# Attention and feed-forward block: work regrouped into three phases, with the maxima transposed on VectorE

## The reference

```python
q = (x @ wq).reshape(bsz, toks, 32, 16)      # 32 query heads of size 16
k = (x @ wk).reshape(bsz, toks, 8, 16)       # 8 key/value groups, 4 query heads each
v = (x @ wv).reshape(bsz, toks, 8, 16)
scores = einsum('bqgrd,bkgd->bgrqk', qg, k) / sqrt(16)
out = einsum('bgrqk,bkgd->bqgrd', softmax(scores), v).reshape(bsz, toks, 512) @ wo
x = layernorm(x + out)
inter = x @ c1_w.T @ c2_w.T                  # rank 16, 1792 columns in blocks of 32
idx = argmax of each block of 32             # one column of each block is kept
h = relu(x . w1[idx]);  out = h @ w2t[idx]
x = layernorm(x + out)
```

## Time and profile before

| | |
|---|---|
| median of 3 runs | 1001.59 us (998.66 to 1003.35) |
| profiled execution | 998.58 us, of which the span from first to last instruction is 996.8 us |
| mean granted TensorE clock | 0.944 of full |
| PE busy | 908.2 us (91%) |
| DVE busy | 562.4 us (56%) |
| ACT busy | 442.9 us (44%) |
| POOL busy | 193.1 us (19%) |
| DMA | 92.99 MB |

### The profile page before, as it was taken

How to read it: one execution, slowest core, us unless ns; L and a number is a source line. 1 busy time by engine, 2 the same in 40 slices (tenths; PEclk the granted TensorE clock), 3 DMA queues, 4 the chain that set the end, 5 groups by cost and what they waited for, 6 DMA issues and landing times. The chain is left out here.

```text
span 996.8 us, 12134 instructions
## 1 busy us (share of the span) xinstructions
PE 908.2 (91%) x4472; PEld 533.0 (53%) x4472; DVE 562.4 (56%) x743; ACT 442.9 (44%) x821; POOL 193.1 (19%) x183
## 2 busy tenths in 40 slices
PE   5868999999899998999989975999999999999995
PEld 3745543333334333343333434777777777777774
DVE  4636567888656885468866533545563365326413
ACT  3302466777654775456765542322222222222231
POOL 6302003730210002100021002333321222122221
PEclk8889999999989998599988978999999999999998
DMA  8466535643342243323433124214030002001101
GB/s 249 160 205 240 169 110 159 175 123 91 91 117 69 76 134 80 97 85 79 135 82 109 34 97 102 82 44 155 14 116 11 1 3 103 2 1 43 42 1 42
DMA packets 50858, 92.99 MB, mean 93 GB/s; under 512 B 5648, under 2 KB 13840, under 8 KB 50288
## 3 DMA queue, kind: packets, MB, share of 16 engines
q1 hardware_dynamic: 49312, 87.05, 29.3%
q0 software_dynamic: 1488, 5.16, 1.9%
HBM read 56.80 MB, written 34.87 MB: 92 GB/s over the span
## 5 line engine op out<-in xcount | busy, mean ns | idle before, releaser
L509 DVE TENSOR_REDUCE neg_max<-ps_max 128x2 f32<-128x1024 f32 x256 | 302.9, 1217 | 90.1 <-PE ps_max L670 89.7
L486 ACT ACTIVATE probs<-ps_st 128x512 f32<-128x512 f32 x496 | 270.2, 595 | 142.6 <-PE ps_st L707 139.7
L707 PE MATMUL ps_st<-q,k 50*128 50x512 f32 x496 | 181.9, 511 | 28.5 <-ACT probs L486 27.6
L707 PEld LDWEIGHTS ps_st<-q,k 50*128 50x128 f32 x496 | 71.9, 192 | 203.1 <-ACT probs L486 156.8
L670 PE MATMUL ps_max<-k,q 48*128 48x512 f32 x512 | 152.8, 452 | 14.0 <-DVE neg_max L509 9.2
L721 PE MATMUL ps_pv<-probs,v 128*32 128x512 f32 x1024 | 147.3, 649 | 5.9 <-ACT probs L486 2.3
L978 POOL TENSOR_TENSOR g_l<-picked,g_h 128x512 fp32r<-128x512 f32 x56 | 73.1, 1306 | 286.9 <-ACT g_h L1017 286.9
L1003 ACT ACTIVATE mask_t<-ps_t 128x512 bf16<-128x512 bf16 x56 | 33.4, 597 | 163.6 <-PE ps_t L1199 163.6
L1211 PE MATMUL ps_h<-xt_h,w_h 128*128 128x512 f32 x224 | 93.8, 419 | 8.0 <-ACT relu L1010 8.0
L1073 DVE TENSOR_REDUCE top<-ps_prep 128x14 f32<-128x448 f32 x62 | 38.6, 623 | 99.0 <-PE ps_prep L1188 98.8
L670 PEld LDWEIGHTS ps_max<-k,q 48*128 48x128 f32 x512 | 75.6, 199 | 28.9 <-DVE neg_max L509 13.5
(11 more groups left out here) (159 smaller groups left out, 1141.2 us busy)
## 6 DMA issues: line engine op xcount, KB each, us to landing
q_stacks<-parts SPq DMA_DIRECT2D x48, 256.0 KB
q<-q_stacks SPq DMA_DIRECT2D x64, 192.0 KB, 3.6
sums<-stage SPq DMA_DIRECT2D x32, 256.0 KB, 3.4
k<-k_stacks SPq DMA_DIRECT2D x64, 96.0 KB, 3.1
x_raw<-xT SPq DMA_DIRECT2D x16, 256.0 KB, 8.5
yf<-after_attention SPq DMA_DIRECT2D x4, 1024.0 KB, 5.3
w_raw<-w POOLq DMA_DIRECT2D x16, 224.0 KB, 3.1
w_raw<-w SPq DMA_DIRECT2D x14, 256.0 KB, 2.9
```

Source lines behind the costliest of these rows:

```text
L486: nc.scalar.activation(probs[kt % 2][:, r], score_bank(n, r), ACT.Exp, scale=float(HD) ** -0.5).then_inc(exp_done, 1)
L509: nc.vector.tensor_reduce(neg_max[n % 2][:, i // 2, :, i % 2], ps_max[i % 2][:], AX.X, ALU.max, negate=True).then_inc(max_red, 1)
L707: nc.tensor.matmul(score_bank(n, r), k_[n % QR][64 * a:64 * a + ROWS, kt * P:(kt + 1) * P], q[n % QR][64 * a:64 * a + ROWS, j, :], start=T ...
```

## The change

The work is regrouped into three phases.

1. *Projections.* All four batches are projected first, with four PSUM banks in rotation (`bank(i)` is one of three `ps_st` or `ps_pv`). The results stay in SBUF (`parts0` to `parts3`, `v0` to `v3`), laid over memory that the later phases use for something else. A unit is then loaded from SBUF to SBUF by 12 transfers instead of 4 from DRAM. Maxima of the first two units run beside the projections of batches 2 and 3.
2. *Attention.* No projection and no output projection stands in the units. `ps_x` is gone; there are three `ps_st` banks. The maxima are transposed by DVE in blocks of 32 by 32 (`turn_max` is now one DVE instruction), and POOL's queue takes them to DRAM and, as two rows for each copy, back into `q`. Scaling and splitting the attention output is kept in this phase for the first batch alone (POOL in units 12 and 14). The splitting of w1 is moved to units 22 to 29. The splitting of wo, c1 and c2 is moved from the start to units 1 to 4.
3. *Feed-forward.* It begins with the output projections of all four batches, mixed with the preparation of the first feed-forward batch. Sums and reciprocals of batches 1 to 3 are loaded there one batch at a time.

In phase 3 the relu output also shares a buffer with `picked`, and w2 has a buffer of its own for all tiles.

The core of the diff:

```diff
-        ps_st = [ps(f"ps_st{j}", [P, S]) for j in range(2)]
+        ps_st = [ps(f"ps_st{j}", [P, S]) for j in range(3)]
         ps_pv = ps("ps_pv", [P, S])
-        ps_x = ps("ps_x", [P, S])
...
+            def load_unit(n):
...
+                src = parts[b][HD * g:HD * (g + 1)].bitcast(F32)
                 for a in range(2):
+                    for c in range(3):
+                        rows = slice(64 * a + HD * c, 64 * a + HD * (c + 1))
+                        sp.dma_start(k_[j][rows].bitcast(F32), src[:, 0, (0, 0, 1)[c]]).then_inc(unit_in[j], DMA)
+                        sp.dma_start(q[j][rows].bitcast(F32), src[:, 1 + a::2, (0, 1, 0)[c]]).then_inc(unit_in[j], DMA)
...
+            def send_shift(n):
+
+                to = maxima[n * TILES * 2 * P:(n + 1) * TILES * 2 * P]
+                pool.wait_ge(max_turned, n + 1)
+                dst = to.rearrange("(c t o x) -> o t c x", c=8, t=TT, o=4)
+                for o in range(4):
+                    pool.dma_start(dst[o], max_rows[32 * o:32 * (o + 1)]).then_inc(max_out, DMA)
+                pool.wait_ge(max_out, 4 * DMA * (n + 1))
+                src = to.rearrange("(a h w) -> a h w", a=2, h=2)
+                if n >= QR:
+                    pool.wait_ge(st_mm, TILES * (n - QR + 1))
+                for a in range(2):
+                    pool.dma_start(q[n % QR][64 * a + SHIFT:64 * a + SHIFT + 2].rearrange("p j t -> p (j t)").bitcast(F32),
+                                   src[a]).then_inc(shift_in[n % QR], DMA)
...
+            def turn_max(n):
+                dve.wait_ge(max_split, n + 1)
+                if n:
+                    dve.wait_ge(max_out, 4 * DMA * n)
+                nc.vector.transpose(max_rows[:], max_parts[:].rearrange("p t a h j -> p (t a h j)").bitcast(F32)
+                                    ).then_inc(max_turned, 1)
...
+                for kt in range(TT):
+                    step = n * TT + kt
+                    for pair in range(2 * step + TILES, 2 * step + 2 + TILES):
+                        if pair < NT // 2:
+                            row_max(pair)
+                        if n + 1 < NU and kt < 2:
+                            (high_max, low_max, turn_max, lambda n: None)[2 * kt + pair % 2](n + 1)
...
+            def scale(b):
+                pool.wait_ge(att_in, REP * DMA * b)
+                pool.wait_ge(inv_in, DMA * b)
+                for r in range(REP):
+                    nc.gpsimd.tensor_tensor(att[:, r], att[:, r], inv[:, r], ALU.mult).then_inc(att_scaled, 1)
+
+            pool.wait_ge(half_set, 1)
+            low_w2(0)
+            scale(1)
+            root(0)
+            scale(2)
+            root(1)
+            scale(3)
+            root(2)
+            root(3)
...
             for t in range(TT):
+                project_out(0, t)
+            project_out(1, 0)
+            project_out(1, 1)
+            front(0)
+            front(1)
...
+            project_out(2, 0)
...
+            inner_up(0, 0, (0, 1, 2, 3))
             turn_mask(0, 0)
+            for t in range(TT):
+                project_out(3, t)
```

More of the change, by code:

```diff
@@ new lines, in _ @@
+            for n in range(NU):
+                if n + 1 < NU:
+                    send_shift(n + 1)
+                if n == 1:
+                    load_raw()
+                if n == 3:
+                    high_raw()
+                if n == 4:
+                    low_raw()
+                if n == 12:
+                    scale()
+                if n == 14:
+                    low_att()
+                for i in range(KT * NC):
+                    if 22 + i // 2 == n:
+                        split_w1(i)
@@ new lines, in _ @@
+            for b in range(1, NB):
+                for o in range(VTASK):
+                    low_task(b, o)
+                    if o == 0:
+                        take_v(b - 1)
+                    if b + 1 < NB and o >= 1:
+                        low_x(b + 1, o - 1)
+                    for pair in pairs_at(b, o):
+                        row_max(pair)
+                for pair in pairs_at(b, VTASK):
+                    row_max(pair)
+                if b == NB - 2:
+                    high_max(0)
+                    low_max(0)
+                    turn_max(0)
@@ L693, in scores_t @@
+                t, j, a = i // 4, i // 2 % 2, i % 2
+                if i == 0:
+                    pe.wait_ge(unit_in[n % QR], LOADS * DMA * (n // QR + 1))
+                if a == 0 and tile >= 4:
+                    pe.wait_ge(max_red, tile // 2 - 1)
+                nc.tensor.matmul(ps_max[tile // 2 % 2][:, a], q[n % QR][64 * a:64 * a + STACK, j, t * P:(t + 1) * P],
+                                 k_[n % QR][64 * a:64 * a + STACK, :], start=True, stop=True).then_inc(max_mm, 1)
             def scores_t(n, kt, r):
@@ L774, in _ @@
+            for b in range(1, NB):
+                for o in range(TASKS):
+                    project(b, o)
+                    if o == 0:
+                        turn_v(b - 1)
+                    for pair in pairs_at(b, o):
+                        scores(2 * pair)
+                        scores(2 * pair + 1)
+            turn_v(NB - 1)
+            scores(2 * TILES)
             for n in range(NU):
-                b, g = n // NKV, n % NKV
                 for kt in range(TT):
+                    step = n * TT + kt
+                    ahead = 4 * step + 2 * TILES + 1
@@ L789, in _ @@
[L789 to L790 removed]
+                    if step:
+                        weigh(*divmod(step - 1, TT))
                     scores_t(n, kt, 2)
[L792 removed]
+                    scores(ahead + 1)
                     scores_t(n, kt, 3)
[L794 to L795 removed]
@@ L929, in _ @@
             load_w2(1)
-            for r in range(REP):
-                sp.dma_start(att[:, r], last.rearrange("(g r h d t) -> r h g d t", r=REP, g=NKV, h=2, d=HD)[r, 0]
-                             ).then_inc(att_in, DMA)
             at = (NB - 1) * NH * S
@@ L991, in _ @@
                         low_w2(m + 1)
[L992 to L994 removed]
+                    if b and m == 1:
+                        root(NB + b - 1)
+            root(2 * NB - 1)
         @block.scalar
@@ L1190, in step, with front, project_out @@
                 last.then_inc(prep_mm, 1)
+            def front(s):
+                step(0, s, front_bank(s), 2)
+            def project_out(b, t):
+                if b:
+                    pe.wait_ge(added, TT * (b - 1) + t + 1)
+                for r in range(REP):
+                    if b and t == 0:
+                        pe.wait_ge(att_split, REP * (b - 1) + r + 1)
+                    for i, (a, w) in enumerate(((att_h, wo_h), (att_h, wo_l), (att_l, wo_h))):
+                        last = nc.tensor.matmul(ps_out[t][:], a[b % 2][:, r, t * P:(t + 1) * P], w[:, r],
+                                                start=(r == 0 and i == 0), stop=(r == REP - 1 and i == 2))
+                last.then_inc(wo_done, 1)
             def turn_mask(b, m):
```

1104 lines of the change are left out of this document (465 added, 639 removed).

## The result

The changed kernel takes 1028.29 us (median of 4 runs, 1016.72 to 1031.66) against 1002.16 of before on the same chip: ratio 1.025, 95% interval 1.016 to 1.033. It is slower, though it is unclear whether by more than 2%; 979 was predicted. The profiled execution took 1030.88 us, its span is 1029.1. These are its stages, cut at the first transposed score product (`ps_st`), at the last one, at the feed-forward's first matmul and at the end of the head (columns as in the earlier trace rows).

What follows compares the result with a forecast made beforehand. It took a unit's step as a PE-ACT loop closed by two score banks, no engine at its rate. Terms 90 + 399 + 6.8 + 105 + 373.7 = 974.5 us of span gave 979, own range 955 to 996.

Steps and rivals of the forecast that it cites:

- the units, 399: Phase 2: 32 units of 12.1 us, 387, plus 12 for interruptions; 483 before.
- the path of the maxima: Phase 2: from DVE's reductions through POOL's two transfer rounds (6.8 us, landings 2.2 each), making a unit 12.1 against 11.2.
- The interruptions: Phase 2: 12 us allowed for POOL's splits of wo, c1, c2, the w1 split and one spread in unit 11.
- The clock: Rival, phase 2: PE standing 3.2 us a unit drops the clock; mean unit 17.2, total 1142 us; chance 0.10.
- The second rival: Phase 2: both landings of the maxima's transfers at 3.1 us, unit 13.9, total 1037 us; chance 0.12.
- The step, 2.66: Phase 2: with three banks `weigh` follows `weigh` after 2.66 us, 3.09 before; with the copy of sums 3.25.
- Phase 1: Projections of all batches: 90 us against 103.5 before, bounds 82 and 100.
- The head: Start of phase 3: 105 us, of it 54 work, 43 PE standing in three stands, 8 half clock; bounds 92 and 115.
- The loop behind it: Rest of phase 3, the feed-forward loop after the head: 373.7 us.
- The first rival, a hidden path,: Phase 2: both landings at 1.75 us or less hide the maxima's path; unit 11.2, total 952 us; chance 0.15.

Runs made afterwards that it cites:

- e13_late_apart: `e11_pool_apart` with DVE's cast, low part and transposition of the maxima put back where the changed kernel has them; 992.74 us (0.988 of before).
- e12_banks_fill: `e9_two_banks` with two more products in every step, ahead of the wait for the exponential, their result overwritten; 1006.87 us (1.002 of before).
- e1_early_turn: Changed kernel with DVE's cast, low part and transposition of the next unit's maxima moved to a unit's start; 986.28 us (0.982 of before).
- e11_pool_apart: `e6_sums16` with w2's first split later, batch 0's sums fetched in four parts and scaled later, POOL's other work cut into pieces; 926.86 us (0.920 of before).
- e9_two_banks: `e4_early_and_den`, but each score product waits for the exponential two places back, as with two banks; 1156.91 us, single executions from 1097.43 to 1167.36.
- e4_early_and_den: `e1_early_turn` plus the load of the denominators ahead of the operand transfers on SP's queue; 971.28 us (0.965 of before).
- e6_sums16: `e4_early_and_den` with the reciprocals' spread on 16 outer blocks, and a batch's sums fetched in 8 transfers in place of 4; 959.0 us (0.954 of before).

## Why the prediction was wrong

- **The step that failed: the units, 399.** The sum let the path of the maxima add 0.9 to each unit, held the clock at 1.00 throughout and allowed 12 us for interruptions. Measured are 447.6 at a clock of 0.84, 48.6 more. `e13_late_apart`, which has the path but not the interruptions, takes 417.1 against 32 x 12.1 = 387. So 30 are the path with what the clock does on it, and 18.5 are interruptions.
- **The interruptions.** 12 us were allowed, 30.5 came (447.6 less 417.1). DVE's wait for the denominators wasn't in the sum: SP's list was counted as a time that fits beside the unit (12 x 0.42), not as a queue in which something urgent stands last. Its removal is worth 21 us of phase 2 (13.6 where the path is hidden). The other 9.5 are POOL's long pieces and the 2 MB, foreseen in kind (in the kernels with a hidden path they are dearer: 387.0 to 359.3).
- **The path's size.** 7.55 against 6.8, in the unit shown and as a mean of the 11 units at full clock of `e13_late_apart`: an issue takes POOL 0.61 in the first round, not 0.53; 0.3 pass before the first one; from the last issue of a round to what waits for it are 2.9 and 2.0, where 2.2 and a hand-over were taken for each. The transposition ends 0.2 earlier than laid out. So a unit at full clock is 12.6, not 12.1, and that is about 15 of the 30 (29 x 0.5). It was named as the likeliest error.
- **The clock.** The other half of the 30, about 16 by the estimate above. The rival bounded it by a stand of 3.2 us, the only one shown in the earlier trace rows; nothing showed that shorter ones were harmless. It falls after 1.11, 1.30 and 1.70, so the 0.9 of the forecast wasn't far below stands that bring it down. The rival's own price was wrong too: 5.08 a step came from two banks, and with three a step at half clock is 4.06.
- **A near number by chance.** The second rival, 1037, comes near 1028. Its two landings of 3.1 didn't come; half clock and the interruptions fill the same sum.
- **The step, 2.66.** Right: 2.67. Two banks cost 1.57 a unit (`e12_banks_fill`).
- **Phase 1.** 93.1 against 90. PE stood 3.9 at 57.5 for a bank of maxima; the start, 5.9, was as laid out.
- **The head.** 103 us for 105 from the phase's first transfer, with its three stands. Batch 1 waited for w2 behind the spread, as laid out. The loop behind it took 377.9 for 373.7.
- **The first rival, a hidden path,** was priced at 11.2 a unit and 952. The early transposition gives 10.9, and with the interruptions and the head mended 927. So the change's plan was sound. The path, 1 to 2 us longer a unit than the steps that cover it, decided the sign: `e1_early_turn` removes it alone and is faster than before.

What isn't settled: how the 16 us of half clock would split in the changed kernel itself, where stands have other causes too, and which stand brings the clock down and which doesn't. `e11_pool_apart` has 31 stands, mostly of 0.5 us, at 0.98.

## What to carry to other kernels

Where a path through transfers sets the length of a unit, cost it from rows of such transfers or as a range, and then add what the stands do to the clock: here the path was worth about 43 us in the units at full clock, and half clock another 16 (`e13_late_apart`). Before forecasting, look for any work that can go ahead on the engine where such a path starts; three instructions moved up on DVE were worth 42 us. Look at what stands last in a queue, not only at its sum. And a loop that closes through another engine with small gaps can hold the clock down for a whole phase, though every row says busy: give it one more buffer, or fill it.

## What the runs showed of the hardware

- In `e9_two_banks` the granted clock stayed at 0.50 for over 500 us with PE shown busy throughout (4.56 us steps with 4.06 us of work); with two more products a step it came back to 1.00. The Trainium skill (TensorE: Matmul & The Clock Gate, A second HAM failure mode: psum-queue depth-cycling) tells of short idle times between groups of matmuls that make the clock go up and down; here it didn't go up again within the phase.
- In the second half of a spread with 8 outer blocks the DMA engines' mean busy share was 0.49 at 128 GB/s (`e4_early_and_den`); with 16 blocks 0.99 at 235 GB/s (`e6_sums16`).
- Small transfers of the maxima landed late beside a large one: the wait of POOL for the first round is 2.28 us in the plain unit above and 6.84 at 276.85, behind the issue of batch 0's 2 MB.
- DVE's small instructions can stretch beside POOL's tensor work, and don't always: in the changed kernel the cast of 128 x 16 took 0.17 to 2.26 us in the nine units where POOL worked on tensors at the same time, and 0.17 in the other 23. In `e4_early_and_den` it took 1.67 at 156.04, where POOL subtracted from 152.27 to 161.8.

```profile
152.27 4.58 POOL L321 TENSOR_TENSOR wo_l<-wo_raw,wo_h 128x2048 fp32r<-128x2048 f32 x1
156.04 1.67 DVE L485 CAST max_parts<-neg_max 128x16 fp32r<-128x16 f32 x1
```
